# The passage from a bidirectional GRU to two scan layers: sum made on GpSimd, one block per image, weights prepared earlier

## The reference

```
xn = layernorm(x)
x_inner, z = split(xn @ w_in.T)
fwd = [gru(f_fw, forward), gru(f_rv, reverse)]                 # 96 + 96 channels
bwd = flip([gru(b_fw, ...), gru(b_rv, ...)] of flipped x_inner)
y = silu(fwd + bwd) * silu(z)
x = x + y @ w_out.T
```

```
p = layernorm(x) @ w_in + b_in ; local = depthwise3x3(p)
mixed = 0.25 * (ema left, right, down, up of local) + local
x = x + layernorm(mixed) @ w_out + b_out
x = x + gelu(layernorm(x) @ w1 + b1) @ w2 + b2
```

## Time and profile before

| | us |
|---|---|
| median of 3 runs | 3248.55 (3248.31 to 3249.37) |
| profiled execution, its own time | 3249.77 |
| profiled execution, span | 3248.0 |
| busy PE, DVE, ACT, POOL | 3007.5, 2528.4, 1750.7, 1044.8 |

### The profile page before, as it was taken

One profiled execution on the slowest core, in us unless ns is written; L12 is line 12 of the kernel. 1 busy time (PEld: TensorE's weight loads), 2 busy tenths in 40 slices (PEclk: granted clock), 3 DMA queues, 4 the chain that ended last, 5 costly groups with the idle time before them and its releaser, 6 DMA issues. The chain is left out here.

```text
span 3248.0 us, 126772 instructions
## 1 busy us (share of the span) xinstructions
PE 3007.5 (93%) x50228; PEld 2288.1 (70%) x50228; DVE 2528.4 (78%) x12081; ACT 1750.7 (54%) x5562; POOL 1044.8 (32%) x2518
## 2 busy tenths in 40 slices
PE   6799999999857989999999999999999998589987
PEld 2366665665513349999999999999999997255654
DVE  5699999999755658888888888888888888597772
ACT  2599999999703154444444444444444445144443
POOL 2377777777600102222222222222222222000000
PEclk9899999999968975555555555555555555689999
DMA  2323333333220000000000000000000000000000
GB/s 63 95 90 117 103 103 115 103 105 116 68 77 20 0 2 4 4 4 4 4 4 4 4 4 4 4 4 4 4 4 4 4 4 4 11 1 1 1 5 15
DMA packets 48217, 104.73 MB, mean 32 GB/s; under 512 B 11305, under 2 KB 18793, under 8 KB 47692
## 3 DMA queue, kind: packets, MB, share of 16 engines
q1 hardware_dynamic: 31756, 45.08, 4.8%
q0 software_dynamic: 13824, 50.34, 4.3%
q10 hardware_dynamic: 2112, 2.05, 0.3%
HBM read 84.06 MB, written 13.37 MB: 30 GB/s over the span
## 5 line engine op out<-in xcount | busy, mean ns | idle before, releaser
L539 PE MATMUL g_zr<-g_hp,g_wp 97*128 97x4 f16 x24576 | 1073.3, 171 | 3.3 <-DVE g_hp L589 3.3
L539 PEld LDWEIGHTS g_zr<-g_hp,g_wp 97*128 97x128 f16 x24576 | 947.9, 107 | 89.1 <-DVE g_hp L589 4.9
L640 POOL COPY s_y<-g_hs 96x8 f32<-96x8 f32 x2048 | 404.7, 198 | 1211.8 <-DVE g_hs L591 1211.8
L627 ACT ACTIVATE g_e<-g_n 96x8 f32<-96x8 f32 x2048 | 358.0, 175 | 560.6 <-DVE g_n L576 560.6
L589 DVE TENSOR_TENSOR_SCAN g_hp<-g_gates,g_e 96x16 f16<-96x16 f32 x2048 | 385.9, 188 | 272.4 <-ACT g_e L627 179.8
L517 PE MATMUL g_zr<-s_inner,g_wi 96*128 96x64 bf16 (+1 forms) x6144 | 571.2, 234 | 3.1 <-DVE g_hs L566 3.1
L624 ACT ACTIVATE g_gates<-g_zr 96x16 f32<-96x16 f32 x2048 | 401.4, 196 | 244.7 <-PE g_zr L539 244.7
L546 PE MATMUL g_n<-g_hp,g_wp 97*128 97x8 f16 x8192 | 520.2, 174 | 0.0
L892 DVE CUSTOM_DVE_ANT_0 a_negated<-a_scores,a_mask 128x1024 f32<-128x1024 f32 x384 | 468.1, 1219 | 60.4 <-PE a_scores L810 60.0
L918 ACT ACTIVATE a_probs<-a_negated,a_negmax 128x1024 f32<-128x1024 f32 x384 | 442.4, 1152 | 18.3 <-DVE a_negmax L892 8.6
L576 DVE TENSOR_TENSOR_SCAN g_n<-g_gates,g_n 96x24 f32<-96x24 f32 x2048 | 420.5, 205 | 7.8 <-ACT g_gates L624 7.8
(11 more groups left out here) (310 smaller groups left out, 3261.3 us busy)
## 6 DMA issues: line engine op xcount, KB each, us to landing
a_mask<-in_L_mask POOLq DMA_DIRECT2D x96, 512.0 KB, 5.5
a_k<-k_rows SPq DMA_DIRECT2D x96, 144.0 KB
a_q<-q_rows SPq DMA_DIRECT2D x96, 72.0 KB
o_parts<-a_o_sb SPq DMA_DIRECT2D x384, 18.0 KB
o_part<-o_parts SPq DMA_DIRECT2D x32, 192.0 KB
q_rows<-r_parts SPq DMA_DIRECT2D x12, 192.0 KB
k_rows<-r_parts SPq DMA_DIRECT2D x4, 576.0 KB, 3.6
out_x<-x SPq DMA_DIRECT2D x4, 384.0 KB, 3.0
```

The lines of the kernel that those rows point to most:

```text
L539: mm = pe.matmul(zr_bank[u, k][:, 1 - g, d, :, at], wp[0:97, part, (2 * u + d) * NG + g, :], hp[u][0:97, d * NB:(d + 1) * NB, e], start=False,
L627: act.activation(e1[u][:, :, 0], tn[u, k][:, :, 2], ACT.Tanh, scale=to_tanh).then_inc(n_and_zh[u], 1)
L640: po.tensor_copy(yv[:, 2 * u:2 * u + 2, :, token:token + 1], h.unsqueeze(3)).then_inc(y_ok[u], 1)
```

## The change

1. The order of the four scans is f_fw, b_rv, b_fw, f_rv, so that the two halves' outputs add position by position. `s_y` has two planes instead of four. In the first 512 steps GpSimd copies as before; from step 512 on it adds the new state to what the other half has written at that token.
2. Behind the loop stands a `recycle`, and then one block for silu, multiplication, projection and residual, image by image, with a PSUM tile for each image.
3. `ema_prepare` is the class `EmaPreparation`. Its ten loads (all on SP), its constants, folding and scaling stand in L1's `layernorm`, at the places marked `extra`; the rest (`scan_matrices`) stands at the front of DVE's list in `project_and_split`. An additional `recycle` stands ahead of that `layernorm`; `load` and the preparation's block are gone from the way to `ema_layers`. The methods hold the instructions of the old block.
4. The fill of the borders of `s_inner` moves on GpSimd from `layernorm` to `project_and_split`, because `s_inner` now lies where the norm's buffers were. The norm's output `xn` lies in `z`.

```diff
-SCANS = ('f_fw', 'b_rv', 'f_rv', 'b_fw')
+SCANS = ('f_fw', 'b_rv', 'b_fw', 'f_rv')
...
                     token = s if u == 0 else L - 1 - s
-                    po.tensor_copy(yv[:, 2 * u:2 * u + 2, :, token:token + 1],
-                                   h.unsqueeze(3)).then_inc(y_ok[u], 1)
+                    to = yv[:, :, :, token:token + 1]
+                    if s < L // 2:
+                        po.tensor_copy(to, h.unsqueeze(3)).then_inc(y_ok[u], 1)
+                    else:
+                        if s == L // 2:
+                            po.wait_ge(y_ok[1 - u], L // 2 + 1)
+                        po.tensor_tensor(to, to, h.unsqueeze(3), ALU.add).then_inc(y_ok[u], 1)
...
def layernorm(...):
+        if extra:
+            block.sync(extra.loads)
         def _(po):
             po.memset(inverse[:, :], 0.0).then_inc(cleared, 1)
+            if extra:
+                extra.constants(po)
         def _(pe):
             ... means and squares of all images
+            if extra:
+                extra.fold(pe)
             pe.wait_ge(inv_ok, 1)
             ... spread
+            if extra:
+                extra.centre_biases(pe)
         def _(ve):
             ... subtraction of the means
+            if extra:
+                extra.scale_weights(ve)
             ve.wait_ge(dev_ok, 1)
             ve.wait_ge(cleared, 1)
             ve.reciprocal(inverse[0:tiles, :], deviation[:, :]).then_inc(inv_ok, 1)
+            if extra:
+                extra.add_folded(ve)
             ... multiplication
+            if extra:
+                extra.take_biases(ve)
         def _(act):
             ... squares
+            if extra:
+                extra.choose(act)
             act.wait_ge(squares_used, NB)
             act.activation(deviation[:, :], var[:, :], ACT.Sqrt, bias=eps[0:tiles]).then_inc(dev_ok, 1)
...
def project_and_split(...):
+        @block.gpsimd
+        def _(po):
+            po.memset(inner[0:C, :, :, :, 0:T], 0.0)
+            po.memset(inner[0:C, :, :, :, L + T:L + 2 * T], 0.0)
+            po.memset(inner[C:C + 2, 1, 0, :, :], 1.0)
+            po.memset(inner[C:C + 2, 1, 1:3, :, :], 0.0)
+
         @block.vector
         def _(ve):
+            ema.scan_matrices(ve)
             for b in range(NB):
...
def gru_block(...):
+            @block.scalar
+            def _(act):
+                for b in range(NB):
+                    for m in range(2):
+                        act.activation(y[:, m, cols(b)], y[:, m, cols(b)], ACT.Silu).then_inc(gated, 1)
+            @block.tensor
+            def _(pe):
+                for b in range(NB):
+                    pe.wait_ge(multiplied, 2 * (b + 1))
+                    for k in range(2):
+                        for m in range(2):
+                            mm = pe.matmul(product[b][:, k * BANK:(k + 1) * BANK], w_out[:, m, :],
+                                           z[:, m, b * L + k * BANK:b * L + (k + 1) * BANK],
+                                           start=(m == 0), stop=(m == 1))
+                    mm.then_inc(projected, 1)
+            @block.vector
+            def _(ve):
+                def add(b):
+                    ve.wait_ge(projected, b + 1)
+                    ve.tensor_tensor(x[:, cols(b)], x[:, cols(b)], product[b][:, :], ALU.add)
+                for b in range(NB):
+                    for m in range(2):
+                        ve.wait_ge(gated, 2 * b + m + 1)
+                        ve.tensor_tensor(z[:, m, cols(b)], z[:, m, cols(b)], y[:, m, cols(b)],
+                                         ALU.mult).then_inc(multiplied, 1)
+                    if b:
+                        add(b - 1)
+                add(NB - 1)
...
class EmaPreparation:
+    def loads(self, sp):
+        for dst, src in self.loads_:
+            sp.dma_start(dst, src).then_inc(self.loaded, 16)
+    def choose(self, act):
+        ... three copies into chosen, one into spread
+    def scale_weights(self, ve):
+        ve.wait_ge(self.loaded, 16 * len(self.loads_))
+        ... 8 tensor_scalar, then 4 tensor_reduce over the weights
+    def scan_matrices(self, ve):
+        for i, w in enumerate(self.layers):
+            for j, t in enumerate((w["w_out"], w["w2"])):
+                ve.tensor_scalar(t[:, :, C], t[:, :, C], 1.0 / C, None, ALU.mult).then_inc(self.meaned, 1)
+        ... 16 tensor_tensor_scan into forth and back
+        for i, w in enumerate(self.layers):
+            for j, (t, n) in enumerate(((w["w_out"], 2), (w["w2"], FT))):
+                ve.wait_ge(self.meaned, 2 * i + j + 1)
+                for s in range(n):
+                    ve.tensor_scalar(t[:, s, 0:C], t[:, s, 0:C], t[:, s, C:C + 1], None, ALU.subtract)
+        ... forth + back, then along_rows and along_columns
```

More of the change, by code:

```diff
@@ L965, in bass_program @@
             gates = retention_block(nc, d, x, v, vector_pairs, mean96, eps6, q_rows, k_rows, o_parts, gates_ctx)
[L966 to L974, removed]
+            ema, pairs = [], []
+            for layer in ("L2", "L3"):
+                w, layer_pairs = ema_weights(nc, ctx, d, layer, v)
+                ema.append(w)
+                pairs += layer_pairs
+            recycle(nc)
+            preparation = EmaPreparation(nc, ctx, ema, pairs)
+            gru_block(nc, x, v, mean96, eps5, gates, preparation)
+        ema_layers(nc, ema, x, d["out"], preparation.matrices())
 CHANNEL_VECTORS = [("L0_" + n, 1) for n in ("pos_b", "ln1_g", "ln1_b", "q_b", "q_b_rot", "k_b", "k_b_rot", "v_b",
@@ L1432, in gru_block @@
         w_out = gates["w_out"]
         recycle(nc)
-        def add(ve, m, b, psum):
-            return ve.tensor_tensor(x[:, cols(b)], x[:, cols(b)], psum, ALU.add)
-        project(nc, "s_out", [z[:, 0, :], z[:, 1, :]], lambda s, m: w_out[:, s, :], 1, C, add, "vector")
+        with ExitStack() as ctx:
+            sem = lambda name: ctx.enter_context(semaphore(nc, "y_" + name))
+            product = [ctx.enter_context(nc.psum_tensor(f"y_product{b}", [C, L], F)) for b in range(NB)]
+            gated, multiplied, projected = sem("gated"), sem("multiplied"), sem("projected")
+            block = ctx.enter_context(nc.Block())
+            @block.scalar
[26 more added lines that the diff above has]
+                add(NB - 1)
@@ new lines, in choose, with fold @@
+    def choose(self, act):
+        act.wait_ge(self.set_up, 1)
+        act.wait_ge(self.filled, 7)
+        for part in PARTS:
+            rows = slice(part, part + 32)
+            act.activation(self.chosen[rows, :], self.ident[rows, part:part + TURNS],
+                           ACT.Copy).then_inc(self.chosen_ok, 1)
+        act.wait_ge(self.chosen_ok, len(PARTS))
+        act.activation(self.spread[:, :, :], self.chosen[:, :].unsqueeze(2).broadcast_to([128, TURNS, 128]), ACT.Copy)
+    def fold(self, pe):
+        pe.wait_ge(self.loaded, 16 * len(self.loads_))
+        for i, w in enumerate(self.layers):
+            raw, to = w["raw"], self.folded[:, i, :]
+            for f in range(FT):
+                pe.matmul(to[:, 3 + f:4 + f], raw["w1"][:, f * 128:(f + 1) * 128], w["n2_b"],
+                          start=(i == 0 and f == 0), stop=True, skip_group_check=True)
+            for m in range(2):
+                pe.matmul(to[0:C, m:m + 1], raw["w_in"][:, m * C:(m + 1) * C], w["n1_b"], start=False, stop=True,
+                          skip_group_check=True)
+            for s in range(2):
+                mm = pe.matmul(to[0:C, 2:3], raw["w_out"][:, s, :], w["on_b"][:, s:s + 1], start=False,
+                               stop=(s == 1), skip_group_check=True)
+        mm.then_inc(self.bias_ok, 1)
@@ new lines, in centre_biases @@
+    def centre_biases(self, pe):
+        pe.wait_ge(self.set_up, 2)
+        pe.wait_ge(self.plain_ok, 4)
+        for i, w in enumerate(self.layers):
+            mm = pe.matmul(self.centred[:, i, :], self.centre[:, :], w["plain"][:, :], start=(i == 0), stop=True,
+                           skip_group_check=True)
+        mm.then_inc(self.centred_ok, 1)
+    def scale_weights(self, ve):
+        ve.wait_ge(self.loaded, 16 * len(self.loads_))
+        for w in self.layers:
+            raw = w["raw"]
+            ve.tensor_scalar(w["w_in"][:, :], raw["w_in"][:, :], w["n1_g"], None, ALU.mult)
+            ve.tensor_scalar(w["w1"][:, :], raw["w1"][:, :], w["n2_g"], None, ALU.mult)
+            for s in range(2):
+                ve.tensor_scalar(w["w_out"][:, s, 0:C], raw["w_out"][:, s, :], w["on_g"][:, s:s + 1], None,
+                                 ALU.mult).then_inc(self.scaled, 1)
+        ve.wait_ge(self.scaled, 4)
+        for w in self.layers:
+            for t in (w["w_out"], w["w2"]):
+                ve.tensor_reduce(t[:, :, C], t[:, :, 0:C], AX.X, ALU.add).then_inc(self.summed, 1)
```

237 lines of the change are left out of this document (86 added, 151 removed).

## The result

| | before | after | ratio, 95% interval |
|---|---|---|---|
| first comparison | 3248.43 us (3248.03 to 3249.37, 4 runs) | 3216.07 us (3214.44 to 3222.85, 4 runs) | 0.9903, 0.9890 to 0.9917 |
| second | 3246.05 us (3242.18 to 3251.43, 7 runs) | 3222.64 us (3220.78 to 3224.84, 4 runs) | 0.9931, 0.9915 to 0.9948 |
| third | 3250.22 us (3248.38 to 3250.43, 9 runs) | 3221.35 us (3217.89 to 3222.21, 5 runs) | 0.9912, 0.9899 to 0.9926 |

The kernel became faster by 32.4, 23.4 and 28.9 us; the forecast was 24.4. The first comparison's 3216.07 lies in the range of 3212 to 3238, but 2 us outside the likeliest case's own range of 3218 to 3230; the medians of the other two lie inside it. The profiled execution of after took 3216.37 us for a span of 3214.3.

A forecast was written before the change was run, and what follows sets the result against it. Bound: serial single-engine stages, 58.8 us between recurrence and layers, after 1024 dependent steps of 1.517 us. Sum -33.5 - 1 + 0.8 + 1.1 - 1 + 9.2 = -24.4, from 3248.55 to 3224.2 us; range 3212 to 3238.

The forecast's parts named there:

- likeliest case: The whole kernel: the summed forecast of 3224.2 us, own range 3218 to 3230 from the parts' bounds, chance 0.68.
- Part 1: Behind the recurrence: one block per image replaces the serial stages; layers start at 25.3 us instead of 58.8, minus 33.5.
- The walk: Output block behind the loop: step-by-step timing from GpSimd's last end to the layers' first matmul, 25.3 us.
- TensorE's cold start: Output projection: the first six matmul instructions run at the low clock, 0.86 us each instead of 0.43.
- The warm start of the layers: Scan layers' first four instructions: 1.7 us instead of 3.7 after a 2.1 us pause; taken as minus 1.
- Part 2: Normalization in front: clearing plus 0.8, later root plus 1.1, clock minus 1; together plus 0.9.
- the root's delay: Normalization: ScalarE's four copies ahead of the table load make the root later, plus 1.1 us (bounds nothing and 1.8).
- minus 1 for both: Normalization clock: folding may save up to 2.4 us, a longer starting pause may cost up to 1; taken as minus 1.
- Part 3: Input projection: GpSimd's border memsets hold VectorE's tensor_scalars and TensorE waits 6.6 us, then restarts slow; plus 9.2 (bounds 0.1 and 11).
- only the ten are held: Input projection: memsets hold only the ten tensor_scalars behind the sixteen scans, so VectorE is free at 14.2 us.
- Part 4: Recurrence: GpSimd's 1024 later copies become adds of 217 ns instead of 198, hidden; cost nothing.
- Rival 3: Recurrence: VectorE's product waits for GpSimd's whole add, 51 to 72 us over 512 steps, about 3284 us; chance 0.07.

The follow-up runs named there:

- experiment 6: Changed kernel with border fills held back, ScalarE's selection behind the root and three unused matmuls ahead of the output block: 3204.18 us, repeated 3203.49 us.
- experiment 2: Changed kernel with loads and whole preparation again behind the recurrence, in a block after the new output block: 3228.81 us, ratio to before 0.9951.
- Experiment 1: Changed kernel with GpSimd's border fills waiting until VectorE has made the last scan matrix: 3211.2 us, ratio to before 0.9894.
- experiment 3: Changed kernel with GpSimd copying in all 1024 steps instead of adding in the second half: 3221.47 us, ratio to before 0.9925.
- experiment 4: Changed kernel and kernel before, each run again unchanged for a second profile: 3222.64 us and 3246.25 us.

## Why the prediction was right

Its sum (-24.4 us) came out because its three rebuilt stages did: forecast -33.5 + 0.9 + 9.2 = -23.4, found -23.6 between the first profiles of each kernel (-24.0 between the second ones). Inside it two errors of 1.6 us, in parts 2 and 3, cancel, which is luck, and the layers' -1 failed. The measured -32.4, -23.4 and -28.9 us also hold what the last point calls not forecast.

- **Part 1 (-33.5).** Right: 25.03 us against 25.3. The walk's inner order was partly off. The silus had the 0.96 us of their own duration (7.68 for eight), not the 1.125 of the earlier trace rows, which had included waits for adds; the multiplications took 1.16. TensorE's cold start came as charged, six instructions at 0.50, and experiment 6 took 1.3 to 2.5 us of it away. The boundary with a clearing was 1.29 us, not 1.1.
- **The warm start of the layers (-1).** Wrong: `e_mix` took 3.70 us as before. TensorE stood still for 1.97 us, and the granted clock was 0.50 from its first instruction on. The term took the high clock as kept over a short pause. The pause's length alone does not decide it here: the clock was 0.50 after these 1.97 us, and 1.00 after 2.8 us in experiment 2.
- **Part 2 (+0.9).** Mis-sized: +2.5 to +3.0. The clearing is 0.77 (1.09 us at the boundary instead of 0.32) and the root's delay 0.97, both near the forecast of 0.8 and 1.1. The term that failed is "minus 1 for both" of the clock. The first subtraction came 1.0 us later (3.08 us after TensorE's start instead of 2.09), but only 0.16 of it was left at the end of the last square (15.25 us instead of 15.09). The folding gave nothing back: the spread instructions took 9.91 us instead of 9.27. So the term was +0.8 between the first profiles. In the second profile of before these two figures were 14.14 and 9.86, so it varies by a microsecond by itself.
- **Part 3 (+9.2).** Right in mechanism and nearly in size: +7.6. The first four tensor_scalars lay beside the two short memsets only and took 0.26 to 0.58 us instead of the 0.16 to 0.17 that they take without, so VectorE was free at 13.5 us, near the "only the ten are held" case (14.2) and not at the 15.3 that I took between two cases. The 0.7 less is what VectorE got done between the two long memsets, ahead of the last hold. TensorE therefore stood still for 4.43 us instead of 6.6, and the six slow instructions behind the pause cost the 2.6 forecast. Experiment 1 shows the hold as the whole cost, by taking it away.
- **Part 4 (nothing).** Right: no cost shows, with 208 ns for the add where I took 217, and with a disturbance of 30 ns that the room absorbs (experiment 3). Rival 3 is refuted.
- **Not forecast:** what the medians show beyond the rebuilt stages' -23.6 us: 8.8 us in the first comparison, nothing in the second, 5.3 in the third, and 10 between the first two profiles. In L0 it is within chance. In the recurrence (2 to 3 us) and the layers (2 to 4 us) all three profiles of after lie below both of before, but one variant's profile lies with those of before in both (1552.2 and 435.7), so it is not fixed by the new code alone. In the layers it is TensorE's time at 0.50 (experiment 4). Whether the buffers' new places, the scans' new order or chance of the execution places these stretches and lengthens the loop was not separated and stays open.

## What to carry to other kernels

Moving work under a stage is paid for by whom it meets there, not by its own length: the moved preparation had its 5 us of room in the projection, and it was the fill that moved into the same block that made it cost 7.4 us. One wait that orders the two gave that back. And where TensorE waits for other engines ahead of a dense stretch of matmuls, its idle time can be filled with matmuls that nothing uses, up to the moment when the real ones come; ahead of the output block this took 1.3 to 2.5 us off.

## What the runs showed of the hardware

- A GpSimd memset over 2 partitions holds VectorE's large tensor_scalar as long as it lasts (groups of two and three: 2.32 beside 3.61, 7.45 beside 7.25 us, for 0.42 and 0.61 alone), but neither its scans (0.20 us, before and beside the 3.61), nor its tensor_tensor of 96x1024 (1.21 beside 7.13). The hold was let go at the boundary between two long memsets (1162.15 to 1162.24), where in the earlier trace rows it lasted over a row of short ones.
- A GpSimd add of 96x8 takes 208 ns, its copy 198; an overlapping VectorE product with two inputs in SBUF lost 30 ns to the add and none to the copy.
- Ahead of the projection TensorE was idle for 2.5 to 2.8 us in twelve profiles. It began at 0.50 in ten of them and at 1.00 in two; in one of these the clock fell during the first instruction, and the next four ran at 0.50, in the other it stayed.
- In the layers TensorE stood at 0.50 for 73 to 92 us, in stretches at different places from profile to profile: 429.0 us long with 73, 436.4 with 92.
- Behind six added matmul instructions at 0.50 (5.2 us) the next 3.5 us ran at 0.98 in one profile; in two others the first two real instructions were still at 0.50 (0.78 over 3.5 us in the one shown).
